# Audio tower with experts: opening loads and fold re-ordered, shared expert's down products moved by one chunk

## The chip, the cores and the metric

One core of one Trainium2 chip runs the whole program. The metric is the device time of one execution in microseconds (us). TensorE (PE in the rows) multiplies, VectorE (DVE), ScalarE (ACT) and GpSimd (POOL) do the rest, SyncE (SP) only issues transfers. ACT and POOL can issue transfers too.

## The reference, cut to what matters

32 audio clips give 250 frames each, so 8000 tokens of 192 numbers.

```python
h = tok(x)                       # |rfft(frame)|^2 @ mel -> log -> @ dct @ w_proj + b_proj
h = h + attn(layernorm(h))       # 8 heads, softmax(q k^T + relative-position bias) v, then a gelu MLP
xn = layernorm(h)
scores = sigmoid(xn @ gate.T)    # 8000 x 16
topk_score, topk_ids = top_k(scores.T, 1000)     # each of 16 experts picks its 1000 best tokens
xg = xn[topk_ids]
out = (silu(xg @ Wg.T) * (xg @ Wu.T)) @ Wd.T * topk_score     # hidden width 768
y = zeros.at[topk_ids].add(out)
shared = (silu(xn @ Ws_g.T) * (xn @ Ws_u.T)) @ Ws_d.T         # hidden width 384
return h + y + shared
```

## The kernel before, in words

Every engine has a program of its own, written out by hand in order. A semaphore is a counter: `then_inc` raises it, `wait_ge` holds the engine, and all that is queued behind on that engine, until a value is reached.

**The tower** (`tower`) runs 32 batches of 250 tokens as a pipeline of five stages; `body(bt, bq, bb_, bc, bd)` is one round with up to five batches in flight, each in eight slots `s`. Stage `bt` is the front end: spectrum (`dft`, slot 1), mel filter (`mel`, slot 2), log, projection (`wmel`, slot 4), layer norm and rms norm (slots 5 and 6), a transpose and a split into a high and a low part, `hsp` (slot 7). Stage `bq` forms q, k, v (`qk`, first matmuls of the next round) and the position terms `rsb`, which SP stores into `bias_d`. That tensor is filled with zeros beforehand, and the first store waits for it (`zero_st`).

Before the first round stands an opening. SP loads `frames` of batch 0, waits for three memsets of POOL, and issues 40 loads on one semaphore, `w_ld`. All other engines wait for all of them (`W_LOADS`). Then come:

- the high half of the weight split on ACT (`wsp` from `wraw`, two operations of 1600 columns) and the low half on DVE;
- the fold on PE: `wqT` by `wpz` (32 half-array matmuls recorded at L742), `dct` by `wproj` into `wmel`, and `wpz` by `vcol` into `cq`;
- four small high copies on ACT and four low ones on DVE of the folded columns.

After `ini` has reached 9, PE starts the spectrum of batch 0.

**The feed-forward part** (`feed_forward`) has 16 chunks of 500 tokens for the shared expert. In a chunk PE does three units (`m`): a gate and an up product, five matmuls each, into the PSUM tiles `gps` and `ups`, two buffers each. ACT takes the silu, DVE multiplies (`gated`) into `s_hT`. Then PE does 24 down matmuls (two groups of 12) from `s_hT` into `dps`, and DVE adds the residual (`added`). ACT then issues the store of the result. The split of the next chunk's input is `high` on ACT and `low` on DVE.

In chunks 0 to 9 the same engines search the 16 thresholds of the top 1000 bit by bit, three steps a chunk. `count` is a DVE pass over 128x1000 scores, `tally` a small matmul that sums it over partitions, `update` three short DVE operations that need the tally. In chunks 10 to 15 (`SEARCH` is 10) `route` turns the thresholds into index lists: prefix sums by a scan on DVE with a matmul behind it on PE (`route(c, 4)`), then `one_hots` on DVE, `list_mm` on PE, `list_out` on DVE. SP stores the list (`store_list`) and loads it back, POOL gathers 1000 rows by eight indirect transfers (`gather`), and PE transposes them (`rows_T`), with `rows_high` on ACT and `rows_in` on DVE, for the first of 16 experts. In SP's own order the store of list 0 stands behind all transfers of the chunks, and the last of those waits for `added(13)`.

After that come 16 turns of an expert each.

## Time and profile before

| what | value |
|---|---|
| three runs | 2084.29, 2087.18, 2087.20 us; median 2087.18 |
| the profiled execution, its own time | 2081.72 us |
| its span, first to last instruction | 2080.1 us |
| busy: PE, DVE, ACT, POOL | 92%, 66%, 51%, 34% of the span |
| opening, until the first q/k matmul | 0 to 46.5 us |
| tower | to about 1088 us |
| shared expert and routing, chunks 0 to 15 | 1094.3 to 1299.7 us |
| first expert's rows | 1299.7 to 1314.1 us |
| 16 expert turns | 1314.1 to 2080 us |

All stages follow one another on PE, so the span is their sum. A busy share over the whole span says little about one stage: what an edit is worth is read inside its stage, from who waits for whom.

### The profile page before, as it was taken

The page shows a single profiled execution, that of the slowest core. Times are in us where ns is not written, and L with a number is a line of the kernel's source. Part 1 is how long each engine was busy: PE and PEld are TensorE (multiplying, and loading weights), DVE is VectorE, ACT ScalarE, POOL GpSimd, SP SyncE. Part 2 cuts the span into 40 slices and gives each one's busy share as a digit, 9 for nine tenths or more (in the row PEclk, how much of TensorE's full clock was granted, in tenths as well). Part 3 has the DMA queues.
Part 4 walks back from the last instruction along what each step waited for, and adds up shares of the span by engine and source line. Part 5 has one row for each costly group of instructions (what it writes and reads, how often), then busy time and mean ns, then how long its engine had stood idle before and what let it go on. Part 6 is the DMA issues. An engine that isn't in the chain of part 4 may idle for free. (4 is left out here: it accounts for less than half of the span.)

```text
span 2080.1 us, 46488 instructions
## 1 busy us (share of the span) xinstructions
PE 1912.6 (92%) x13428; PEld 1634.6 (79%) x13428; DVE 1364.8 (66%) x3748; ACT 1070.9 (51%) x2588; POOL 704.5 (34%) x587
## 2 busy tenths in 40 slices
PE   2899999999999999999958899799999999999997
PEld 2688888888888888888847787688888888888886
DVE  2577878878878878878746777455555555555531
ACT  2687787887887887887732221222222222222221
POOL 0122222222222222212210002266666665566663
PEclk9999999999999999999979999899999999999999
DMA  5666666666766666666636333244454554444451
GB/s 154 167 164 174 186 172 173 188 170 172 191 168 172 193 166 175 188 167 178 189 89 164 98 99 90 64 81 82 82 93 83 99 99 83 79 78 81 81 95 19
DMA packets 318048, 272.95 MB, mean 131 GB/s; under 512 B 80732, under 2 KB 305326, under 8 KB 317998
## 3 DMA queue, kind: packets, MB, share of 16 engines
q1 hardware_dynamic: 238878, 235.53, 42.1%
q0 software_dynamic: 70656, 30.65, 10.2%
q10 hardware_dynamic: 8464, 6.15, 0.9%
q8 instruction: 26, 0.43, 0.1%
q14 instruction: 24, 0.20, 0.0%
HBM read 151.25 MB, written 120.54 MB: 131 GB/s over the span
## 5 line engine op out<-in xcount | busy, mean ns | idle before, releaser
L1211 POOL DMA_INDIRECT out<-ff_y,ff_idxs x128 | 261.8, 2045 | 232.7 <-DVE ff_y L1490 175.0
L1266 ACT ACTIVATE ff_sg<-ffp_g 128x500 f32<-128x500 f32 x192 | 113.0, 589 | 384.5 <-PE ffp_g L1602 384.5
L1198 POOL DMA_INDIRECT ff_xg<-xs_d,ff_idxg x128 | 206.3, 1612 | 284.4 <-issue 269.4
L524 ACT ACTIVATE sb_prob<-sb_ssb,sb_mx 125x250 f32<-125x250 f32 x512 | 253.3, 499 | 61.0 <-DVE sb_rinv L614 33.1
L1614 PE MATMUL ffp_d<-ff_wd,ff_wide 128*125 128x192 f32 x1536 | 261.2, 327 | 7.7 <-DVE ff_wide L1477 6.7
L1477 DVE TENSOR_TENSOR ff_wide<-ff_sg,ffp_u 128x500 f32<-128x500 f32 x192 | 129.4, 674 | 207.9 <-PE ffp_u L1602 207.9
L1602 PE MATMUL ffp_g<-ff_xsp,ff_wsp 128*128 128x500 f32 x960 | 250.8, 391 | 7.6 <-issue 6.0
L1614 PEld LDWEIGHTS ffp_d<-ff_wd,ff_wide 128*125 128x125 f32 x1536 | 247.8, 188 | 11.2 <-issue 9.1
L1602 PE MATMUL ffp_u<-ff_xsp,ff_wsp 128*128 128x500 f32 x960 | 250.1, 390 | 0.0
L1602 PEld LDWEIGHTS ffp_g<-ff_xsp,ff_wsp 128*128 128x128 f32 x960 | 180.1, 189 | 45.3 <-issue 9.5
L822 PE MATMUL ps_qps<-sb_hsp,sb_wsp 128*128 128x250 f32 x1280 | 184.5, 291 | 32.0 <-DVE sb_hsp L728 22.8
L1602 PEld LDWEIGHTS ffp_u<-ff_xsp,ff_wsp 128*128 128x128 f32 x960 | 181.4, 189 | 37.2
L822 PEld LDWEIGHTS ps_qps<-sb_hsp,sb_wsp 128*128 128x128 f32 x1280 | 159.5, 191 | 56.8 <-ACT sb_rsb L510 28.2
L608 DVE CUSTOM_DVE_ANT_0 sb_ssb<-ps_sps,sb_bsk 125x250 f32<-125x250 f32 x512 | 192.0, 412 | 10.1 <-PE ps_sps L773 3.2
L510 ACT ACTIVATE sb_rsb<-ps_qps 125x502 f32<-125x502 f32 x256 | 137.0, 590 | 80.4 <-PE ps_qps L844 66.2
L587 DVE COPY sb_ptsb<-ps_ptps 125x500 f32<-125x500 f32 x256 | 170.8, 667 | 5.0 <-PE ps_ptps L784 3.0
L784 PE MATMUL ps_ptps<-sb_ident,sb_prob 125*125 125x125 f32 x1024 | 154.8, 273 | 2.3 <-ACT sb_prob L524 1.4
L773 PE MATMUL ps_sps<-sb_kk,sb_qu 64*125 64x250 f32 x1024 | 143.3, 398 | 0.2
L455 POOL TENSOR_TENSOR sb_t_y<-sb_t_v,sb_power 125x4 f32<-125x4 f32 x32 | 33.0, 1032 | 323.8 <-DVE sb_t_v L711 323.8
L784 PEld LDWEIGHTS ps_ptps<-sb_ident,sb_prob 125*125 125x125 f32 x1024 | 136.9, 188 | 5.1 <-ACT sb_prob L524 2.6
L1241 ACT ACTIVATE ff_xsp<-ffp_tp 128x500 fp32r<-128x500 f32 x64 | 37.6, 587 | 175.7 <-PE ffp_tp L1525 175.7
L1490 DVE TENSOR_SCALAR ff_y<-ffp_d,ff_gsc 125x192 f32<-125x192 f32 x128 | 47.5, 413 | 119.3 <-PE ffp_d L1614 119.3
(190 smaller groups left out, 3528.0 us busy)
## 6 DMA issues: line engine op xcount, KB each, us to landing
bias_d<-sb_rsb SPq DMA_DIRECT2D x256, 219.6 KB
sb_bsk<-bias_d SPq DMA_DIRECT2D x256, 218.8 KB
hx_d<-sb_hx SPq DMA_DIRECT2D x32, 336.0 KB
sb_hxl<-hx_d SPq DMA_DIRECT2D x32, 336.0 KB
ff_wd<-WdT SPq DMA_DIRECT2D x16, 576.0 KB, 5.0
xs_d<-sb_xs SPq DMA_DIRECT2D x32, 238.0 KB
bias_d<-sb_rsb SPq DMA_DIRECT2D x256, 25.5 KB
sb_bsk<-bias_d SPq DMA_DIRECT2D x256, 25.4 KB
```

The lines of the kernel that those rows point to most:

```text
L510: a.activation(rsb[:, h % 2], bank2(qps[R_USE[h] % 2], NDE, TP)[:, :, 0:ND], ACT.Copy).then_inc(q_ev[R_USE[h] % 2], 2)
L524: a.activation(prob[:, s % 2, t], ssb[:, s % 2, t], ACT.Exp, bias=mx[:, s % 2, t:t + 1], scale=-1.0, accum_out=rs[:, t, s:s + 1]).then_inc ...
L587: v.tensor_copy(ptsb[:, h % QUAD], ptps[:]).then_inc(pt_ev, 1)
L608: v.tensor_tensor_reduce(out=ssb[:, s % 2, t], in0=sps[s % 2][:, t], in1=bsk[:, s % 4, t], scale=-SCALE, scalar=3.0e38, op0=ALU.add, op1=A ...
L773: ins = m(sps[i][:, t], qu[rows, p, t * TP:(t + 1) * TP], kk[rows, p], start=True, stop=True)
L784: ins = nc.tensor.transpose(ptps[:, j, t * TP:(t + 1) * TP], prob[:, h % 2, t, j * TP:(j + 1) * TP], ident[0:TP, 0:TP])
L822: ins = m(ps[:, i], wsp[:, wk, col:col + 128], hsp[:, xp, xk], start=k == 0, stop=k == len(PARTS) - 1)
L1198: g.indirect_dma_start(xg[:, t], None, xs_d[:, :], bass.IndirectOffsetOnAxis(idxg[:, t:t + 1], 0), bounds_check=last).then_inc(gat, 16)
L1211: g.indirect_dma_start(out_d[:, :], bass.IndirectOffsetOnAxis(idxs[:, t:t + 1], 0), y[:, t], None, bounds_check=last, compute_op=ALU.add). ...
L1477: v.tensor_tensor(hT[:, m, half * HALF:(half + 1) * HALF], sg[:, n % 2], ups[n % 2][:], ALU.mult).then_inc(h_ev, 1)
L1602: ins = m_(ps[n % 2][:], wsp[:, i, wk, m * 128:(m + 1) * 128], xsp[:, xp, xk, half * HALF:(half + 1) * HALF], start=k == 0, stop=k == 4)
L1614: ins = m_(dps[j % 2][:, i], hT[:, m, t * TP:(t + 1) * TP], wd[:, m], start=m == 0, stop=m == ME - 1)
```

## The change

In the opening the loads fall into four semaphores: `f_ld` (`dft`), `t_ld` (what the first front end reads), `w_ld` (weights to be split and folded) and `l_ld` (what only later stages read). Twelve loads of `wq`, `wk`, `wv`, `w1` become three of one array, `wall`, joined on the host. ACT issues 12 loads itself. The front end of batch 0 starts when its own few loads are there; the weight split and the fold stand behind its steps on each engine. The fold's PSUM tiles are `cps` and `otps` in place of `tps` and `cps`. The zero stores stand behind all loads, the POOL memset of `zeros` behind the others.

In the feed-forward part `down(c-1)` stands behind the first unit of chunk c, `added(c-1)` and the store with it, and DVE's order within a chunk is another. `list_mm` and some `one_hots` move. The first expert's four transposed groups get four PSUM tiles (`rows_ps`).

The diff, cut to its core:

```diff
@@ tower, SP @@
+            loads = [(wraw[:, 0], w["wall"][0:128])] + [(wraw[64 * i:64 * i + 64, 1], w["wall"][128:D]) for i in range(2)]
+            ...  braw x4, ucol;   late = wo, w2, gate, n2w, b1, bb x4
             load_frames(0)
-            sp.wait_ge(z_set, 3)
+            sp.dma_start(mel[0:BINS], w["melT"]).then_inc(t_ld, 16)
+            sp.dma_start(mel[BINS:2 * BINS], w["melT"]).then_inc(t_ld, 16)
+            sp.wait_ge(z_set, 2)
             for dst, src in loads:
                 sp.dma_start(dst, src).then_inc(w_ld, 16)
+            sp.wait_ge(t_mm, 1)
+            load_frames(1)
+            for dst, src in late:
+                sp.dma_start(dst, src).then_inc(l_ld, 16)
+            sp.wait_ge(z_set, 7)
@@ tower, ACT @@
+            act.dma_start(dft[:], w["dft"]).then_inc(f_ld, 16)
+            ...  dct, wproj, wmel on t_ld;  wqT, vcol, wpz x4 on w_ld;  ident, n1w on t_ld
             a.preload_act_table_set(EXP_SET)
-            act.wait_ge(w_ld, W_LOADS)
             act.wait_ge(z_set, 7)
...
                         a.activation(hx[:, :, 0:D], bank2(tps, D, TP), ACT.Copy).then_inc(t_ev, 1)
+                        if opening(bt):
+                            weights_high()
@@ tower, DVE: weights_low() behind h1n @@
+                        if opening(bt):
+                            weights_low()
@@ tower, PE @@
                         m(tps[0:2 * BINS, 0:FRAMES], dft[:], frames[:], start=True, stop=True).then_inc(t_mm, 1)
+                        if opening(bt):
+                            mel_fold()
...
                         ins.then_inc(t_mm, 1)
+                        if opening(bt):
+                            fold()
@@ tower, PE, qk of batch 0 @@
+                    if opening(b):
+                        pe.wait_ge(ini, 8)
@@ feed_forward, first expert's rows @@
+            if isinstance(e, int) and e == 0:
+                return (tp, gps[0], gps[1], ups[0])[j][:, 0:HALF].rearrange("p (t n) -> p t n", n=TP)
@@ feed_forward, ACT, chunk @@
-                if not last:
-                    high(c + 1, 1 - par)
+                    if m == 0 and (not isinstance(c, int) or c < CHUNKS - 1):
+                        high(c + 1, 1 - par)
+                    if m == 0 and (not isinstance(c, int) or c > 0):
+                        stored(c - 1, 1 - par)
@@ feed_forward, DVE, chunk @@
+                    if c == SEARCH:
+                        update(STEPS * c - 1)
+                    route(c, 0)
+                    if c < CHUNKS - 1:
+                        low(c + 1, 1 - par)
+                    if c == SEARCH + 4:
+                        list_out(0)
+                    added(c - 1, 1 - par)
+                    gated(c, par, 0)
+                    for m in range(1, MS):
                         route(c, m)
                         gated(c, par, m)
                     route(c, 3)
-                    if c < CHUNKS - 1:
-                        low(c + 1, 1 - par)
-                    added(c, par)
                 else:
+                    if not first:
+                        update(STEPS * c - 1)
                     count(STEPS * c)
-                    gated(c, par, 0)
                     update(STEPS * c)
                     count(STEPS * c + 1)
+                    low(c + 1, 1 - par)
+                    if not first:
+                        added(c - 1, 1 - par)
+                    if first:
+                        gated(c, par, 0)
+                    update(STEPS * c + 1)
+                    if not first:
+                        gated(c, par, 0)
+                    count(STEPS * c + 2)
                     gated(c, par, 1)
-                    update(STEPS * c + 1)
                     gated(c, par, 2)
-                    count(STEPS * c + 2)
-                    low(c + 1, 1 - par)
-                    update(STEPS * c + 2)
-                    added(c, par)
@@ feed_forward, PE, chunk, behind unit m @@
                     if search and m == 0:
                         tally(STEPS * c)
+                    if not search and c == SEARCH + 4 and m == 0:
+                        list_mm(0)
+                    if m == 0 and not first:
+                        down(c - 1)
+                    if search and m == first:
+                        tally(STEPS * c + 1)
                     if search and m == 2:
-                        tally(STEPS * c + 1)
+                        tally(STEPS * c + 2)
                     if not search:
                         route(c, m)
-                pe.wait_ge(s_h_ev, MS * (c + 1))
-                ...  24 down matmuls
                 if not search:
                     route(c, 4)
```

DVE in the opening, before: the split and the fold's copies (`sb_wsp`, `sb_bz`, `sb_cq`) lead, the norm of batch 0 (`sb_t_stats` and on) follows.

```order
L569 CAST sb_bz<-sb_braw 128x504
L572 TENSOR_TENSOR sb_wsp<-sb_wraw,sb_wsp 128x1600
L572 TENSOR_TENSOR sb_wsp<-sb_wraw,sb_wsp 64x1600
L574 COPY sb_cq<-ps_qps 128x4
L575 COPY sb_wmel<-ps_qps 40x192
L579 TENSOR_TENSOR sb_wsp<-ps_tps,sb_wsp 128x4x32
```

And of the change, from the last part of that norm to the split of batch 0's `hsp`:

```order
L759 TENSOR_SCALAR sb_h1n<-sb_hx,sb_t_y 125x64
L604 CAST sb_bz<-sb_braw 128x504
L607 TENSOR_TENSOR sb_wsp<-sb_wraw,sb_wsp 128x1600
L607 TENSOR_TENSOR sb_wsp<-sb_wraw,sb_wsp 64x1600
L609 COPY sb_cq<-ps_qps 128x4
L613 TENSOR_TENSOR sb_wsp<-ps_cps,sb_wsp 128x4x32
L613 TENSOR_TENSOR sb_wsp<-ps_otps,sb_wsp 128x4x32
L613 TENSOR_TENSOR sb_wsp<-ps_cps,sb_wsp 64x4x32
L613 TENSOR_TENSOR sb_wsp<-ps_otps,sb_wsp 64x4x32
L766 SCALAR_TENSOR_TENSOR sb_hsp<-ps_tps,sb_n1w,sb_hsp 128x250 x2
```

The whole split now stands between `h1n` and `hsp` of batch 0.

PE at the end of chunk 10, the first behind the search, before: units 1 and 2 (`ffp_g`, `ffp_u`), the down products (`ffp_d`), then the prefix matmul (`ff_before`), then chunk 11.

```order
L1567 MATMUL ffp_g0<-sh_s_xsp,sh_s_wsp 128x500 x5
L1567 MATMUL ffp_u0<-sh_s_xsp,sh_s_wsp 128x500 x5
L1580 MATMUL ffp_d0<-sh_s_wd,ff_s_hT 125x192 x6
L1580 MATMUL ffp_d1<-sh_s_wd,ff_s_hT 125x192 x6
L1542 MATMUL ffp_kl<-ff_wide,ff_before 128x1
L1567 MATMUL ffp_g1<-sh_s_xsp,sh_s_wsp 128x500 x5
```

And of the change:

```order
L1648 MATMUL ffp_g0<-sh_s_xsp,sh_s_wsp 128x500 x5
L1648 MATMUL ffp_u0<-sh_s_xsp,sh_s_wsp 128x500 x5
L1618 MATMUL ffp_kl<-ff_wide,ff_before 128x1
L1648 MATMUL ffp_g1<-sh_s_xsp,sh_s_wsp 128x500 x5
L1648 MATMUL ffp_u1<-sh_s_xsp,sh_s_wsp 128x500 x5
L1635 MATMUL ffp_d0<-sh_s_wd,ff_s_hT 125x192 x6
```

The prefix matmul now follows unit 2 at once; the down products of chunk 10 stand behind it and behind the first unit of chunk 11.

DVE from the end of chunk 13 into chunk 14, before (`ff_lst` and `ff_lsti` are `list_out(0)`, `ff_y` is `added(13)`, `sh_s_xsp` is `low(14)`):

```order
L1334 TENSOR_TENSOR ff_val<-ff_one_lo,ff_tile 125x64x32
L1310 TENSOR_TENSOR sh_s_xsp<-sh_s_xraw,sh_s_xsp 128x500 x2
L1317 TENSOR_TENSOR ff_y<-ffp_d0,ff_res 125x384
L1317 TENSOR_TENSOR ff_y<-ffp_d1,ff_res 125x384
L1341 COPY ff_lst<-ffp_kl 32x64
L1344 TENSOR_TENSOR ff_lst<-ffp_kl,ff_lst 32x64 x3
```

And of the change (`sh_s_xsp` is now `low(15)`):

```order
L1399 TENSOR_TENSOR ff_val<-ff_one_lo,ff_tile 125x64x32
L1375 TENSOR_TENSOR sh_s_xsp<-sh_s_xraw,sh_s_xsp 128x500 x2
L1406 COPY ff_lst<-ffp_kl 32x64
L1409 TENSOR_TENSOR ff_lst<-ffp_kl,ff_lst 32x64 x3
L1412 SCALAR_TENSOR_TENSOR ff_lsti<-ff_lst 32x32
L1382 TENSOR_TENSOR ff_y<-ffp_d0,ff_res 125x384
L1382 TENSOR_TENSOR ff_y<-ffp_d1,ff_res 125x384
```

`added(13)` now stands behind `list_out(0)` and waits for the down products behind it on PE. SP's order at this place is the same in both kernels.

## Rows read from the trace of the kernel before

**Rows 1.** Windows: busy us per engine, granted clock, DMA share, GB/s.
```profile
0.00:25.00 25.00, 0.00 (x0) 0.00 (x0) 0.00 (x0) 1.28 (x1) 2.43 (x11) 1.00 0.56 148
```

**Rows 2.** Timeline of the opening: start, us, engine, line, operation.
```profile
21.41 1.73 SPq L349 DMA_DIRECT2D sb_wraw<-w  x3
23.19 7.04 SPq L353 DMA_DIRECT2D bias_d<-sb_zeros  x5
25.24 2.96 ACT L470 ACTIVATE sb_wsp<-sb_wraw 128x1600 fp32r<-128x1600 f32 x2 [23.08 <-DMA sb_wraw<-w]
26.81 3.68 DVE L572 TENSOR_TENSOR sb_wsp<-sb_wraw,sb_wsp 128x1600 fp32r<-128x1600 f32 x2 [1.15 <-ACT sb_wsp L470]
29.60 1.87 PE L745 MATMUL ps_qps<-sb_vcol,sb_wpz 128*128 128x1 f32 x8
```

**Rows 3.** Timeline: the first front end and the first q/k product.
```profile
33.40 1.16 PE L866 MATMUL ps_tps<-sb_frames,sb_dft 100*102 100x250 f32 x2 [1.93 <-DVE sb_wsp L579]
...
35.02 1.06 PE L872 MATMUL ps_tps<-sb_sq,sb_mel 102*40 102x250 f32 x2 [0.47 <-ACT sb_sq L528]
...
38.48 0.49 ACT L546 ACTIVATE sb_hx<-ps_tps 125x384 f32<-125x384 f32 x1 [0.43 <-PE ps_tps L897]
...
43.25 0.26 DVE L723 TENSOR_SCALAR sb_h1n<-sb_hx,sb_t_y 125x64 f32<-125x64 f32 x1
...
45.56 0.86 DVE L728 SCALAR_TENSOR_TENSOR sb_hsp<-ps_tps,sb_n1w,sb_hsp 128x250 fp32r<-128x250 f32 x2 [2.05 <-ACT sb_hsp L560]
46.47 2.21 PEld L822 LDWEIGHTS ps_qps<-sb_hsp,sb_wsp 128*128 128x128 f32 x10 [2.21 <-DVE sb_hsp L728]
...
53.26 13.16 SPq L98 DMA_DIRECT2D bias_d<-sb_rsb  x12
```

**Rows 4.** Windows: the first 2.5 us behind the loads, zero stores running.
```profile
25.00:27.50 2.50, 2.24 (x22) 2.24 (x22) 1.11 (x2) 2.26 (x2) 0.00 (x0) 1.00 0.99 271
```

**Rows 5.** Transfers by line: KB each, median us to landing.
```profile
bias_d<-sb_zeros SPq DMA_DIRECT2D x5, 779.7 KB, 10.8
sh_s_xraw<-xnT_d SPq DMA_DIRECT2D x16, 250.0 KB, 4.4
```

**Rows 6.** Waits, chunks 1 to 9: us in total, times, longest.
```profile
PE ffp_d L1580 <- DVE ff_s_hT L1304: 11.6, 9, 1.3
```

**Rows 7.** Timeline of PE: one search chunk and the next one's start.
```profile
1199.67 1.44 PE L1567 MATMUL ffp_g<-sh_s_xsp,sh_s_wsp 128*128 128x500 f32 x5
...
1208.48 2.21 PE L1580 MATMUL ffp_d<-sh_s_wd,ff_s_hT 128*125 128x192 f32 x12 [1.32 <-DVE ff_s_hT L1304]
...
1212.56 1.43 PE L1567 MATMUL ffp_g<-sh_s_xsp,sh_s_wsp 128*128 128x500 f32 x5
```

**Rows 8.** Timeline of DVE: a count and a prefix scan.
```profile
1105.75 1.25 DVE L1289 TENSOR_SCALAR_CACHE_REDUCE ff_wide<-ff_wide,ff_cand 128x1000 f32<-128x1000 f32 x1
...
1233.41 2.23 DVE L1383 TENSOR_TENSOR_SCAN ff_wide<-ff_wide 128x1000 f32<-128x1000 f32 x1
```

**Rows 9.** Timeline of PE: first matmuls of chunks 1, 10 and 14.
```profile
1109.79 1.43 PE L1567 MATMUL ffp_g<-sh_s_xsp,sh_s_wsp 128*128 128x500 f32 x5
...
1225.41 1.43 PE L1567 MATMUL ffp_g<-sh_s_xsp,sh_s_wsp 128*128 128x500 f32 x5
...
1275.32 1.41 PE L1567 MATMUL ffp_g<-sh_s_xsp,sh_s_wsp 128*128 128x500 f32 x5
```

**Rows 10.** Timeline, SP, POOL, PE: list 0, its gather, the first expert's rows.
```profile
1276.68 0.34 SPq L1145 DMA_DIRECT2D idx_d<-ff_lsti  x1
...
1283.27 3.36 POOL L1198 DMA_INDIRECT ff_xg<-xs_d,ff_idxg  x1 [194.80 <-issue]
...
1286.93 1.32 POOL L1198 DMA_INDIRECT ff_xg<-xs_d,ff_idxg  x1 [0.30 <-issue]
...
1303.79 1.07 PE L1525 MATMUL ffp_tp<-ff_ident,ff_xg 125*128 125x125 f32 x4 [4.04 <-DMA ff_xg<-xs_d,ff_idxg]
...
1314.08 2.42 PE L1602 MATMUL ffp_g<-ff_xsp,ff_wsp 128*128 128x500 f32 x5 [1.55 <-DVE ff_xsp L1354]
```

More of the change, by code:

```diff
@@ L205, in tower @@
         zero_st = sem("zero_st")
+        t_ld = sem("t_ld")
+        f_ld = sem("f_ld")
+        l_ld = sem("l_ld")
+        mel_mm = sem("mel_mm")
+        mel_in = sem("mel_in")
         fold_mm = sem("fold_mm")
@@ L736, in _, with mel_fold, fold @@
             m = nc.tensor.matmul
-            pe.wait_ge(w_ld, W_LOADS)
-            for p in range(PAIRS):
-                for k in range(2):
-                    for i in range(2):
-                        rows = slice(64 * i, 64 * i + 64)
-                        m(folded(i, k)[:, p], wqT[rows, p, k * 128:(k + 1) * 128], wpz[rows, p, 0, i], start=True, stop=True)
-            m(qps[1][0:MELS, 0:D], dct[:], wproj[:], start=True, stop=True)
-            for p in range(PAIRS):
-                ins = m(qps[0][:, p:p + 1], wpz[:, p].rearrange("d r i n -> d (r i n)"), vcol[:, p:p + 1], start=True, stop=True)
-            ins.then_inc(fold_mm, 1)
-            pe.wait_ge(ini, 9)
-            pe.wait_ge(z_set, 7)
+            pe.wait_ge(f_ld, 16)
+            pe.wait_ge(z_set, 7)
+            def mel_fold():
+                pe.wait_ge(t_ld, T_LOADS)
+                m(qps[1][0:MELS, 0:D], dct[:], wproj[:], start=True, stop=True).then_inc(mel_mm, 1)
+            def fold():
+                pe.wait_ge(w_ld, W_LOADS)
+                for p in range(PAIRS):
+                    for k in range(2):
+                        for i in range(2):
+                            rows = slice(64 * i, 64 * i + 64)
+                            m(folded(i, k)[:, p], wqT[rows, p, k * 128:(k + 1) * 128], wpz[rows, p, 0, i], start=True, stop=True)
+                for p in range(PAIRS):
+                    ins = m(qps[0][:, p:p + 1], wpz[:, p].rearrange("d r i n -> d (r i n)"), vcol[:, p:p + 1], start=True, stop=True)
+                ins.then_inc(fold_mm, 1)
             def transposes(ps, src, s):
@@ L1240, in rows_high, with stored @@
                 k, half = j % 2, j // 2
-                a.activation(xsp[:, 0, k, half * HALF:(half + 1) * HALF], tps.rearrange("p t n -> p (t n)"), ACT.Copy).then_inc(t_hi, 1)
+                a.activation(xsp[:, 0, k, half * HALF:(half + 1) * HALF], rows_ps(e, j).rearrange("p t n -> p (t n)"), ACT.Copy).then_inc(t_hi, 1)
+            def stored(c, par):
+                act.wait_ge(s_y_ev, 2 * c + 2)
+                sprayed(act, out_d[bass.ds(c * CHUNK, CHUNK), :].rearrange("(t p) n -> p t n", p=TP), y[:, CT * par:CT * par + CT], y_st[par])
             def chunk(c, par):
-                last = isinstance(c, int) and c == CHUNKS - 1
                 for m in range(MS):
@@ L1551, in route, with down @@
                     places(1)
-                if c == SEARCH + 3 and place == 4:
-                    list_mm(0)
-                if c == SEARCH + 5 and place == 4:
-                    list_mm(1)
+            def down(c):
+                pe.wait_ge(s_h_ev, MS * (c + 1))
+                for i in range(2):
+                    wait(pe, s_y_ev, 2 * (c - 1) + i + 1)
+                    for t in range(2):
+                        for m in range(MS):
+                            ins = m_(dps[i][:, t], s_hT[:, m, (2 * i + t) * TP:(2 * i + t + 1) * TP], s_wd[:, m], start=m == 0, stop=m == MS - 1)
+                    ins.then_inc(s_d_mm, 1)
             def chunk(c, par):
@@ L1587, in _ @@
             chunks(pe, chunk)
+            down(CHUNKS - 1)
+            list_mm(1)
             pe.wait_ge(r_ch, 13)
```

147 lines of the change are left out of this document (82 added, 65 removed).

## The prediction

> **What bounds the kernel now.** I read the windows first, then the timeline of the opening, then the waits, the timelines and the chain of waits from chunk 0 to the first expert. PE is the engine to follow: in the tower's rounds and in the expert turns it is nearly always busy and the diff leaves both as they are, so what stands ahead of them shifts them one for one. Three places are left.
>
> The opening. For 25 us no compute engine does anything but memsets while the transfers move 148 GB/s [rows 1], though they move 271 GB/s as soon as large ones queue [rows 4]. So the opening waits for SP's issues: the last weight load is issued at 21.41 and three issues take 1.73, 0.58 us each; everything starts at 25.24 [rows 2]. The weight work then takes until 33.40, the front end until 46.47 [rows 3].
>
> The chunks. In chunks 1 to 9 PE waits once a chunk, ahead of the down products, for the last product of that chunk: 11.6 us in nine times [rows 6]. The row at 1208.48 shows 1.32 of it, in a chunk of 12.89 us (1199.67 to 1212.56) [rows 7].
>
> The first expert's rows. List 0 is stored at 1276.68, the gather starts at 1283.27, its rows reach PE at 1303.79, and the first expert product starts at 1314.08 [rows 10]. PE's chunk work has ended at about 1299.7. The last wait there is the transfer of the gathered rows, so from here back the chain runs over POOL and SP, not over PE.
>
> **Term 1, the opening.** The first front end now needs only its own loads (`t_ld`). ACT issues 12 loads, the last of them on `t_ld`; at 0.5 us each (0.58 in rows 2 is for large ones) from 0.9 they are out at 7. A transfer of 250 KB lands 4.4 us after its issue [rows 5]; these are small but share the engines with `wall`, so 3.5: landed at 10.5. Bounds: 9, if nothing is in the way; 13, if they land behind all 2.6 MB of `t_ld` and `w_ld` together, which at 271 GB/s [rows 4] take 9.6 us from about 2.5, plus a landing of about 1. A page warns of the upper one: the Trainium skill, "DMA: Bandwidth & Descriptors", section "Issuing engines are not separate DMA queues", says that two issuing engines share the same 16 transfer engines and save only issue time. By that sentence alone the sum would be 2.5 us later.
>
> From `t_ld` on: `mel_fold` and its copy 1.2 (estimate, one small matmul of 1.06 as at 35.02 less overlap, and a DVE copy); mel matmul to `hx` 3.46 (35.02 to 38.48); `hx` to the end of `h1n` 5.03 (38.48 to 43.51) [rows 3]. Then DVE does what it did ahead: cast 0.4, low split 3.68 [rows 2], the folded columns. For these I have the bound of 1.9 (from the fold's end at 31.5 [rows 2] to 33.40 [rows 3], ACT's part included) and take 1.2, since ACT's part is done by then. Last `hsp` to the first q/k product, 0.91 [rows 3]. Sum 15.9: the product starts at 26.4 instead of 46.47, **20.1 us less**. ACT's high split (2.96) and PE's fold (25.26 to 31.5) [rows 2] start when `hx` is formed and end 6 to 7 us later, under DVE's 10 us: free. `w_ld` may land as late as 15.7 at no cost.
>
> The zero stores are issued after that, by 18 us, and need 14.4 us for 3.9 MB at 271 GB/s [rows 4]; one lands 10.8 us after issue [rows 5]. They end near 30. The first `rsb` store needs them 6.8 us behind the first q/k product (46.47 to 53.26) [rows 3], at 33.2. Covered, by 3 us only.
>
> **Term 2, search chunks.** Without its wait a chunk is 12.89 - 1.32 = 11.57 us of PE [rows 7]. What is late next: the first tally stands ahead of the down products, and its count comes on DVE behind the last `gated` (0.6), the last `update` (about 0.6) and the pass of 1.25 [rows 8]. Counted from the chunk's first matmul it is there at 2.70; PE has done unit 0 at 2.41 and waits 0.3. The chain after it (update, count, `low`, `added`, update, `gated`, count, `gated`) ends at 10.8 by the same durations, ahead of unit 2's end. Chunk: 11.7 to 11.85, so 1.1 less. Chunk 0 loses its down products to chunk 1 (4.1 and the wait) but pays 1.4, because `gated(0)` stands behind `low(1)` and its transfer: chunk 1 starts at 1105.8 instead of 1109.79 [rows 9]. Over chunks 1 to 9, 10.0 to 10.5. Chunk 10 starts at 1211.4 instead of 1225.41 [rows 9]; 4 of the 14 are only postponed.
>
> **Term 3, routing chunks.** Chunks 10 to 13 took 49.9 us [rows 9]. Now the prefix matmul of chunks 10 and 11 follows unit 2 directly, and it needs `gated(c, 2)` (0.6) and the scan (2.2 [rows 8]) first; the down products, which hid the scan, come after. PE waits 3.0 us twice, where it waited 0.77. A chunk without tallies is 11.15: 14.25 + 14.15 + 11.9 (transposes) + 11.1 = 51.4. **The gain shrinks here**: chunk 14 starts at 1262.8 instead of 1275.32.
>
> **Term 4, the first expert.** In chunk 14 unit 0 ends at 2.4, `list_mm(0)` waits for the last one-hot until 3.0 and ends at 3.7, `down(13)` ends at 7.65 and `added(13)` at 8.3. SP has the store of list 0 queued behind the residual load of chunk 15, which waits for `added(13)`; so the list, formed by 5.4, is stored at 9.4 and not at 1.4 as before. That is 1272.2 against 1276.68, 4.5 us less. Store to rows is 27.1 us (1276.68 to 1303.79) [rows 10] and nothing in it changes: rows at 1299.3. PE is through with chunk 15 at about 1293 and waits 6 us; whatever PE gained beyond 4.5 us, and the delay of `gated(15, 2)` by a one-hot of 2.2, is lost or hidden there. The four groups then run in four PSUM tiles: instead of 10.29 us (1303.79 to 1314.08) PE, ACT and DVE overlap, 1.1 + 0.6 + 4 x 0.7 + 0.3 = 4.9. First expert product at 1304.2: **9.9 us less** for terms 2 to 4 together.
>
> **Sum.** 20.1 + 9.9 = 30.0. The profiled execution took 2081.72, its span 2080.1, so it would be 2051.7. It was 5.5 us below the median of the three runs (2087.18), which gives 2057; I say **2056**.
>
> **Rivals.**
> - Search chunks stay near 12.9 us because the ring count, tally, update closes on DVE and PE in turn. For it: DVE's work in a chunk is nearly 10 us and four of its steps wait for PE. Against: 1 us of slack as counted. Then store and rows come 10 us later, 20 us less in all: 2067. Chance 0.11.
> - The opening gives only about 11: loads land at 13 and later, or the zero stores end past 33 and hold the first bias. 2066. The transfer rows [rows 4, 5] leave 3 us to that. Chance 0.12.
> - The gather is shorter. The record at 1283.27 took 3.36, the next 1.32 [rows 10]; the long one began while a one-hot of 2.3 us ran on DVE, and there are two such. If the one-hots of chunk 15 fall beside it: 3.9 less, 2052. I count both again inside the gather, so chance 0.12. The Trainium skill, "SBUF — State Buffer", section "Who interferes with whom", infers that a `tensor_tensor` of DVE does not hold descriptor writing on GpSimd; the rows look otherwise, and the rows decide.
> - Nothing gained: the opening ends later for a load I count as free and the chunks give back the rest, within 4 us of now. I find no row for it: 0.03.
> - Slower: the input load of chunk c+2 is issued only behind `added(c-1)`, and the ring is load, `high`, `low`, `added`, again load. I count 9.5 us with a landing of 4.4 [rows 5]. It binds from a landing of 6.6; each us more costs one per chunk. To eat 30 us over ten chunks it must be 9.6: the same transfer would have to land twice as late. 2095. Chance 0.02.
>
> The forecast itself, 26 to 33 us less, has 0.60. So faster by over 0.2% (4 us, about what a measurement of this kernel can tell) 0.94, within it 0.03, slower 0.03. Range 2048 to 2066: the lower end takes the short gather and the early loads with 4 us of spread between runs, the upper the two costlier rivals.
>
> **What would show it.** First q/k matmul near 26.4 (9 to 13 for the loads makes 24.9 to 28.9), with its last wait on DVE's `hsp`. Zero stores landed ahead of the first `rsb` store. Chunk to chunk 11.7 in the search; the wait of `ffp_d` for `ff_s_hT` gone, one of `ffp_kl` for DVE's count of 0.3 in its place. PE waits of 3 us ahead of the prefix matmuls of chunks 10 and 11. Store of list 0 about 9.4 us into chunk 14, PE idle 6 us ahead of the first expert's rows, and 5 us from the rows to its first product. Wrong if the first tally or the zero stores wait for microseconds, or if rows come by another chain than store, load back, gather.

## The result, and the profile after

Four runs of each kernel: the change 2068.03 us median (2067.60 to 2070.41), before 2085.73 (2082.90 to 2087.20), ratio 0.9919, 95% interval 0.9902 to 0.9936. That is 17.7 us less where 30 were forecast, and above the range. The profiled execution of the change took 2068.2 us, its span 2066.5; against the 2051.7 that the sum gave for a profiled execution it is 16.5 us too long. The profiled execution of before lies 5.5 us below the median of its first three runs, that of the change at its own median. So the two traces differ by 13.6 us where the medians differ by 17.7: the times say what the change is worth, the traces say where.

The opening, timeline of the change (start, us, engine, line, operation, and in brackets idle time and what ended it). It answers to [rows 2, 3]:

```profile
3.81 5.05 ACTq L485 DMA_DIRECT2D sb_wpz<-w_pos  x4
8.90 1.75 ACTq L486 DMA_DIRECT2D sb_ident<-ident  x1
10.68 0.65 ACTq L487 DMA_DIRECT2D sb_n1w<-n1w  x1
...
19.33 0.85 PE L780 MATMUL ps_qps<-sb_wproj,sb_dct 13*40 13x192 f32 x2 [14.66 <-DMA sb_n1w<-n1w]
...
34.59 2.46 PE L867 MATMUL ps_qps<-sb_hsp,sb_wsp 128*128 128x250 f32 x10 [5.05 <-DVE sb_hsp L766]
...
41.49 0.79 SPq L98 DMA_DIRECT2D bias_d<-sb_rsb  x2
```

And its windows (busy us of PE, PEld, DVE, ACT, POOL, granted clock, DMA share, GB/s), against [rows 1]:

```profile
5.00:7.50 2.50, 0.00 (x0) 0.00 (x0) 0.00 (x0) 0.00 (x0) 0.00 (x0) 1.00 1.06 294
7.50:10.00 2.50, 0.00 (x0) 0.00 (x0) 0.00 (x0) 0.00 (x0) 0.00 (x0) 1.00 1.05 190
10.00:12.50 2.50, 0.00 (x0) 0.00 (x0) 0.00 (x0) 1.13 (x1) 0.00 (x0) 1.00 1.03 185
```

ACT's last two loads, `ident` (64 KB) and `n1w` (1 KB), are among those that the first front end needs, and they are issued at 8.9 and 10.7 us, behind four issues of 1.26 each. `t_ld` is complete 8 us behind the last of them, while the 16 transfer engines are full (share above 1; that this is the cause is shown by `e10_free` below). The trace names `n1w`, the last one issued, as what ended the wait; `ident` stands just ahead on the same semaphore and may have landed last. From `t_ld` on the sum holds: 15.3 us to the first q/k product (15.9 forecast), 6.9 from there to the first `rsb` store.

From chunk 0 to the first expert, the longest waits of PE (us in total, times, longest):

```profile
PE ffp_tp L1601 <- DMA ff_xg<-xs_d,ff_idxg: 4.4, 1, 4.4
PE ffp_kl L1618 <- DVE ff_wide L1448: 3.0, 1, 3.0
PE ffp_kl L1621 <- DVE ff_wide L1460: 2.9, 1, 2.9
PE ffp_kl L1583 <- DVE ff_wide L1354: 2.9, 9, 0.5
PE ffp_d L1635 <- DVE ff_s_hT L1369: 2.7, 1, 2.7
PE ffp_u L1648 <- DVE ff_s_hT L1369: 2.4, 1, 2.4
```

The nine waits of up to 1.3 of [rows 6] are gone, nine of 0.3 on average stand in their place, as forecast. New and not forecast is the 2.4 in chunk 1. Its timeline shows a transfer behind it:

```profile
1093.14 0.59 SPq L1202 DMA_DIRECT2D ff_wd<-WdT  x1
1094.16 0.34 SPq L1217 DMA_DIRECT2D sh_s_xraw<-xnT_d  x1
1095.04 1.17 SPq L1219 DMA_DIRECT2D sh_s_xraw<-xnT_d  x2
...
1105.21 1.13 ACT L1288 ACTIVATE sh_s_xsp<-sh_s_xraw 128x500 fp32r<-128x500 f32 x2 [7.24 <-DMA sh_s_xraw<-xnT_d]
...
1109.07 1.75 PE L1648 MATMUL ffp_u<-sh_s_xsp,sh_s_wsp 128*128 128x500 f32 x5 [2.37 <-DVE ff_s_hT L1369]
```

The input of chunk 2 is issued behind five constants and 2.1 MB of expert weights that SP loads in chunk 1, and lands 9 us after its last issue. In the order of before nothing on PE hung on it so early; now `low(2)` stands ahead of `added(0)` and `gated(1, 0)` on DVE.

The routing chunks, and the end of the feed-forward part, against [rows 9, 10]:

```profile
1221.34 0.35 PE L1618 MATMUL ffp_kl<-ff_wide,ff_before 128*128 128x1 f32 x2 [3.01 <-DVE ff_wide L1448]
1221.55 1.59 PE L1648 MATMUL ffp_g<-sh_s_xsp,sh_s_wsp 128*128 128x500 f32 x5
1222.94 2.29 PE L1648 MATMUL ffp_u<-sh_s_xsp,sh_s_wsp 128*128 128x500 f32 x5
...
1237.46 2.43 PE L1648 MATMUL ffp_g<-sh_s_xsp,sh_s_wsp 128*128 128x500 f32 x5
...
1262.44 1.30 PE L1648 MATMUL ffp_g<-sh_s_xsp,sh_s_wsp 128*128 128x500 f32 x5
...
1270.98 0.83 SPq L98 DMA_DIRECT2D ff_res<-h_d  x2
1271.86 0.35 SPq L1206 DMA_DIRECT2D idx_d<-ff_lsti  x1
1278.29 3.01 POOL L1259 DMA_INDIRECT ff_xg<-xs_d,ff_idxg  x1 [200.05 <-issue]
1281.61 1.31 POOL L1259 DMA_INDIRECT ff_xg<-xs_d,ff_idxg  x1 [0.30 <-issue]
...
1297.70 1.07 PE L1601 MATMUL ffp_tp<-ff_ident,ff_xg 125*128 125x125 f32 x4 [4.42 <-DMA ff_xg<-xs_d,ff_idxg]
1302.79 1.38 PE L1683 MATMUL ffp_g<-ff_xsp,ff_wsp 128*128 128x500 f32 x5 [1.55 <-DVE ff_xsp L1419]
```

A group of five products takes 1.3 us at full clock and 2.3 to 2.4 behind the 3-us waits. There the windows show half of the clock granted, 1.2 instead of 2.4 GHz:

```profile
1237.50:1241.70 4.20, 4.20 (x11) 3.43 (x12) 2.74 (x5) 1.60 (x3) 0.00 (x0) 0.50 0.00 0
```

Chunk 14 starts 178.5 us behind the start of chunk 0, where before took 181.0 and 168.5 were forecast. The list is stored 9.4 us into chunk 14, as forecast to a tenth; rows to first product 5.1 (4.9 forecast, 10.3 before).

### The profile page after: what moved, and what is told of

It reads as the page before. It is cut to its first block and busy times, and to the rows that moved or that the text cites. A ratio compares the mean times of both kernels' runs of the same rounds, so it can differ in the third digit from the quotient of the medians.

```text
span 2066.5 us, 46500 instructions
## 1 busy us (share of the span) xinstructions
PE 1919.8 (93%) x13428; PEld 1642.8 (79%) x13428; DVE 1364.0 (66%) x3748; ACT 1071.7 (52%) x2588; POOL 700.3 (34%) x587
## 3 DMA queue, kind: packets, MB, share of 16 engines
q0 software_dynamic: 70656, 30.65, 10.3%
## 5 line engine op out<-in xcount | busy, mean ns | idle before, releaser
L1695 PEld LDWEIGHTS ffp_d<-ff_wd,ff_wide 128*125 128x125 f32 x1536 | 247.8, 188 | 14.2 <-issue 13.0
```

The costliest lines, as they stand in the source:

```text
L1695: ins = m_(dps[j % 2][:, i], hT[:, m, t * TP:(t + 1) * TP], wd[:, m], start=m == 0, stop=m == ME - 1)
```

## The experiments

Before, the change and 15 further kernels in one table. The times (us) are of each profiled execution: `t_ld` complete, first q/k product, first `rsb` store, start of chunk 0, then counted from chunk 0: list 0 stored, first rows on PE, first expert product. The ratio to before goes by several executions of each kernel, run side by side; in parentheses stands its 95% interval.

| kernel | t_ld | q/k | rsb | chunk 0 | list | rows | expert | ratio |
|---|---|---|---|---|---|---|---|---|
| before | - | 46.5 | 53.3 | 1094.3 | 182.3 | 209.4 | 219.7 | 1 |
| the change | 19.3 | 34.6 | 41.5 | 1083.9 | 187.9 | 213.8 | 218.9 | 0.9919 |
| e1e_open | 19.6 | 34.9 | 42.1 | 1087.8 | 182.5 | 207.2 | 217.1 | 0.9955 (0.9941 to 0.9970) |
| e2e_shared | - | 46.6 | 53.3 | 1094.1 | 185.8 | 211.6 | 216.7 | 0.9987 (0.9976 to 0.9998) |
| e15_down | - | 46.7 | 53.6 | 1096.6 | 188.5 | 214.3 | 224.5 | 1.0023 (1.0011 to 1.0034) |
| e9_tiles | 18.9 | 34.2 | 41.1 | 1082.7 | 188.5 | 213.4 | 222.5 | 0.9953 (0.9940 to 0.9966) |
| e3e_first | 15.6 | 30.9 | 38.1 | 1084.2 | 189.0 | 214.8 | 219.8 | 0.9912 (0.9894 to 0.9931) |
| e4e_hold | 18.8 | 34.1 | 43.2 | 1087.7 | 188.8 | 213.7 | 217.6 | 0.9923 (0.9908 to 0.9937) |
| e11_rows | 15.0 | 30.3 | 37.7 | 1080.0 | 188.7 | 214.4 | 219.4 | 0.9904 (0.9886 to 0.9922) |
| e10_free | 4.9 | 26.0 | 37.9 | 1079.5 | 185.9 | 211.7 | 216.7 | 0.9890 (0.9876 to 0.9905) |
| e13_zero | 4.9 | 25.9 | 32.9 | 1078.0 | 185.6 | 211.3 | 216.3 | 0.9888 (0.9870 to 0.9906) |
| e5_input | 20.4 | 35.6 | 42.6 | 1085.0 | 184.4 | 209.3 | 213.2 | 0.9916 (0.9902 to 0.9929) |
| e6_prefix | 20.3 | 35.6 | 42.7 | 1088.9 | 179.7 | 205.7 | 210.8 | 0.9886 (0.9869 to 0.9903) |
| e7_list | 19.8 | 35.0 | 41.9 | 1087.0 | 185.0 | 213.1 | 217.3 | 0.9918 (0.9904 to 0.9931) |
| e8_all | 15.7 | 30.9 | 37.8 | 1083.2 | 171.5 | 196.6 | 200.8 | 0.9834 (0.9818 to 0.9850) |
| e12_best | 14.2 | 29.5 | 37.4 | 1082.7 | 171.0 | 195.8 | 199.7 | 0.9809 (0.9796 to 0.9822) |
| e14_best | 4.9 | 25.6 | 32.3 | 1073.5 | 171.1 | 195.8 | 199.7 | 0.9805 (0.9787 to 0.9822) |

### Which part gave what

`e1e_open` and `e2e_shared` each take one of the two functions from the change:

```diff
@@ e1e_open: tower and host arrays of the change, feed_forward of before @@
@@ e2e_shared: tower and host arrays of before, feed_forward of the change @@
```

> Before's feed-forward part behind the change's tower: the opening alone. Theory (the parts add): the first q/k product starts near 34.6 us and chunk 0 near 1084 instead of 1094.3, and nothing behind it moves, so 10.4 us less than before, ratio 0.995. Rival (the opening's gain is partly lost again later, since zero stores and late loads disturb the tower): less than 8 us. Rival (the other part owns most of the gain): within 3 us of before.

> Before's tower in front of the change's feed-forward part: the shared expert, the lists and the four PSUM tiles alone. Theory: first expert product 0.9 us less after the start of chunk 0 and expert turns 2.3 us shorter through the warmer clock, so 3 us less than before, ratio 0.9985, with the input wait of chunk 1 (it takes 14.9 instead of 12) and the half clock in the routing chunks as in the change. Rival (the change's feed-forward part is worth the 9.9 us of the forecast, and the earlier opening cost it the rest): 8 to 10 us less, ratio near 0.996.

`e9_tiles` is the change without the four PSUM tiles, `e15_down` the same feed-forward part behind the tower of before:

```diff
-            if isinstance(e, int) and e == 0:
-                return (tp, gps[0], gps[1], ups[0])[j][:, 0:HALF].rearrange("p (t n) -> p t n", n=TP)
             return tps
@@ PE, ahead of each group @@
-                if not isinstance(e, int) or e > 0:
-                    pe.wait_ge(t_ev, TR * e + j)
+                wait(pe, t_ev, TR * e + j)
```

> The change with the first expert's four transposed groups back in one PSUM tile, in turn. Theory (within the feed-forward part the four tiles carry the gain, and the moved down products by themselves bring the rows no earlier): rows to first expert product 10.3 instead of 5.1 us, and its first products at half clock again, 5 to 7.5 us more than the change: ratio to before 0.9950. Rival (the tiles give little, because ACT and DVE set the pace of the split): at most 2 us more, ratio below 0.993.

> Before's tower, and the change's feed-forward part with the first expert's rows back in one PSUM tile: the moved down products, list and one-hots alone. Theory (what they gain in the search chunks they give back in chunks 1 and 10 to 12 and in the late store of the list): rows as in e2b_shared, 2 us later than before relative to chunk 0, 2 to 4 us slower than before, ratio 1.0015. Rival (they are worth what the ratios of the change, of the opening alone and of the change without the tiles leave, nothing): ratio 0.9995 to 1.0005. Rival (as forecast, 5 us faster without the tiles): 0.9975.

The opening alone gives 0.9955 (0.995 expected), the feed-forward part 0.9987 (0.9985 expected): both first theories hold. The interval of `e1e_open` reaches to 0.9970, so its rival of less than 8 us (0.9962) is unlikely and not excluded. The tiles are worth what 0.9953 and 0.9919 differ by, 7 us, and again 7.5 between 1.0023 and 0.9987. The end of `e15_down`:

```profile
1310.95 0.99 PE L1543 MATMUL ffp_tp<-ff_ident,ff_xg 125*128 125x125 f32 x4 [4.36 <-DMA ff_xg<-xs_d,ff_idxg]
1313.40 1.09 PE L1543 MATMUL ffp_tp<-ff_ident,ff_xg 125*128 125x125 f32 x4 [1.46 <-DVE ff_xsp L1362]
...
1321.16 2.42 PE L1625 MATMUL ffp_g<-ff_xsp,ff_wsp 128*128 128x500 f32 x5 [1.55 <-DVE ff_xsp L1362]
```

10.2 us from rows to first product, and that product at half clock, as in [rows 10]. So the moved down products, with the lists and one-hots moved along, make the kernel **slower**, by 0.23%: PE's search chunks are shorter, but the list is stored 6 us later relative to chunk 0, and the rows hang on the list.

### Why t_ld was late

`e3e_first` issues `ident` and `n1w` ahead of the weights; `e4e_hold` leaves ACT's order as in the change and holds SP's late loads until `t_ld` is complete.

```diff
@@ e3e_first, ACT @@
+            act.dma_start(ident[:], w["ident"]).then_inc(t_ld, 16)
+            act.dma_start(n1w[:], w["n1w"]).then_inc(t_ld, 16)
             act.wait_ge(z_set, 1)
             act.dma_start(wqT[:], w["wqT"].rearrange("(p r) n -> r p n", r=128)).then_inc(w_ld, 16)
@@ e4e_hold, SP (alone) @@
             load_frames(1)
+            sp.wait_ge(t_ld, T_LOADS)
             for dst, src in late:
```

> The change, with ident and n1w issued by ACT ahead of wqT, vcol and the four wpz loads. Theory A (the small loads of the first front end came late because they stood at the end of ACT's own order): they are out by 3.8 us, t_ld is complete near 13, the weights (w_ld) near 20 are next, and the first q/k product starts at 28 to 30 instead of 34.6: 5 us less than the change, ratio to before 0.9895. Theory B (all 16 transfer engines were full and the order of issue does not matter): t_ld complete at 17 or later, at most 2 us less than the change.

> The change, with SP holding its nine late loads back until t_ld is complete; ACT's order is left. Theory C (the late loads of SP, issued from 7.6 us on, took the transfer engines from n1w): t_ld complete near 15 instead of 19.3, first q/k product near 30.5, 4 us less than the change, ratio to before 0.990. Theory A (ACT's order alone): t_ld still near 19, and the zero stores, now issued behind it, end some 5 us later, near 41, where the first rsb store is due at 41.5: same as the change, or up to 2 us slower.

`e10_free` adds to `e3e_first` a wait for `t_ld` ahead of all weight loads; `e11_rows` adds to `e3e_first` one transfer for `wpz` instead of four; `e13_zero` is `e10_free` with the zero stores first.

```diff
@@ e10_free, ACT and SP @@
             act.wait_ge(z_set, 1)
+            act.wait_ge(t_ld, T_LOADS)
...
             sp.wait_ge(z_set, 2)
+            sp.wait_ge(t_ld, T_LOADS)
             for dst, src in loads:
@@ e11_rows, ACT @@
-            for i in range(2):
-                for r in range(2):
-                    act.dma_start(wpz[64 * i:64 * i + 64, :, r, i], ...).then_inc(w_ld, 16)
+            act.dma_start(wpz[:], w["w_pos"].rearrange("q (p r i n) -> q p r i n", p=PAIRS, r=2, i=2)).then_inc(w_ld, 16)
@@ e13_zero, SP: the loop over late stands behind the zero stores @@
```

> The change with ident and n1w first, and all transfers of w_ld (SP's and ACT's) held back until t_ld is complete. Theory (what the first front end reads lands late because the 16 transfer engines are full of weights): t_ld complete at 6 to 8 us instead of 15.6 with the order alone, then w_ld near 20 to 22 is the last wait, the first q/k product at 29 to 31: same time as with the order alone. Rival (these small loads are slow by themselves, each with its own fixed cost): t_ld complete at 12 or later.

> The change with ident and n1w first, and wpz loaded in one transfer with its zeros, 128 rows of 2 KB from an array that the host pads, instead of four transfers of 256 pieces of 128 bytes. Theory (the small pieces hold the transfer engines at 190 GB/s where they could move 290): t_ld complete near 12 instead of 15.6, w_ld near 16 instead of 19.9, first q/k product 27.5 instead of 30.9, 3 us less than with the order alone. Rival (wall and wqT fill the engines, the small pieces are 0.13 MB of 2.6): less than 1 us.

> As e10_free (ident and n1w first, weights held back until t_ld is complete), with SP issuing the zero stores ahead of the nine late loads. Theory (with the first q/k product at 26 the zero stores are the next wait: the first rsb store went 11.9 us behind it instead of 6.9): they are issued near 11 instead of 17.8, the first rsb store goes near 33 to 34 instead of 37.9, and the time is 3 to 4 us less than e10_free, ratio to before 0.987. Rival (the zero stores share the engines with the weights, w_ld lands later and the q/k product with it): first q/k product near 29, first rsb store 36, at most 1.5 us less than e10_free.

Order alone brought `t_ld` from 19.3 to 15.6, in `e3e_first`:

```profile
15.58 0.85 PE L780 MATMUL ps_qps<-sb_wproj,sb_dct 13*40 13x192 f32 x2 [10.84 <-DMA sb_n1w<-n1w]
```

That lies between its two theories (13, and 17 or later). The first q/k product came 3.7 us earlier, but the time moved from 0.9919 to 0.9912 only, less than the intervals can tell and far from the 0.9895 expected. Holding SP's late loads left `t_ld` at 18.8, at the edge of what six traces with the same order of ACT's loads show without that hold (18.9 to 20.4), and its first `rsb` store went 1.7 us later than that of the change. One transfer for the small pieces of `wpz` gave 0.6 us (15.0), and 1.4 in `e12_best` (14.2) against `e8_all` (15.7): the first theories of both fell. The last small load of `e3e_first` was issued at 3.0, and `t_ld` still took 12 us more. With the engines free (`e10_free`) it is complete at once:

```profile
4.87 0.86 PE L782 MATMUL ps_qps<-sb_wproj,sb_dct 13*40 13x192 f32 x2
...
11.06 1.05 PE L923 MATMUL ps_tps<-sb_sq,sb_mel 102*40 102x250 f32 x2 [5.34 <-ACT sb_sq L556]
...
17.59 2.96 ACT L496 ACTIVATE sb_wsp<-sb_wraw 128x1600 fp32r<-128x1600 f32 x2 [2.58 <-DMA sb_ucol<-u]
...
17.78 8.35 SPq L363 DMA_DIRECT2D bias_d<-sb_zeros  x5
...
25.95 2.46 PE L869 MATMUL ps_qps<-sb_hsp,sb_wsp 128*128 128x250 f32 x10 [1.98 <-DVE sb_hsp L768]
...
37.86 1.69 SPq L98 DMA_DIRECT2D bias_d<-sb_rsb  x4
```

So the small loads were late because of the megabytes on their way beside them: that is what the theory of full engines said (6 to 8 us expected, 4.9 measured). The weights lose nothing by starting 3 us later (`w_ld` complete at 17.6, 19.9 in `e3e_first`). There the theory was too careful: it had `w_ld` at 20 to 22 and the product no earlier than with the order alone, and the first q/k product starts at 25.95, 4.9 us ahead of `e3e_first` and 20.5 ahead of before. Of the 14.5 us by which `t_ld` is ahead of the change, 8.6 reach that product. The row at 11.06 shows where most of the rest goes: ACT now issues its weight loads, until 9.3 us, ahead of its first step of the front end, and PE waits 5.3 us for that step. Then the zero stores are late: the first `rsb` store goes 11.9 us behind the product instead of 6.9. `e13_zero` mends that:

```profile
10.56 6.05 SPq L361 DMA_DIRECT2D bias_d<-sb_zeros  x5
...
25.94 2.47 PE L869 MATMUL ps_qps<-sb_hsp,sb_wsp 128*128 128x250 f32 x10 [1.98 <-DVE sb_hsp L768]
...
32.85 6.96 SPq L98 DMA_DIRECT2D bias_d<-sb_rsb  x8
```

The store goes 5 us earlier, as its theory said, but chunk 0 starts only 1.5 us earlier, and the time does not tell the two apart (0.987 expected). The first rounds of the tower, which take the rest back, are below, under the hardware.

### The chunks

```diff
@@ e5_input, SP, chunk: input of chunk c+1 right behind the residual load of chunk c @@
                 sprayed(sp, res[:, par], h1_d[own, :].rearrange("(t p) n -> p t n", p=TP), r_ld[par])
+                if not isinstance(c, int) or c < CHUNKS - 1:
+                    load_x(c + 1, 1 - par)
                 if isinstance(c, int) and c == 1:
@@ e6_prefix, PE, chunk, behind unit m @@
+                    if m == 0 and not search and c - 1 in (SEARCH, SEARCH + 1):
+                        route(c - 1, 4)
                     if m == 0 and not first:
                         down(c - 1)
...
-                if not search:
-                    route(c, 4)
@@ e7_list, SP, chunk @@
+                if isinstance(c, int) and c == CHUNKS - 1:
+                    store_list(0)
+                    load_idx(idxg, ig_ld, 0)
                 wait(sp, s_y_ev, 2 * (c - 1))
```

> The change, with SP issuing the input of chunk c+1 right behind the residual load of chunk c, so that the input of chunk 2 no longer stands behind the constants and expert weights that SP loads in chunk 1; all else as in the change. Theory (chunk 1 waits 2.4 us and then runs at half clock because that input is issued late): chunk 1 takes 12 instead of 14.9 us, chunks 2 to 9 stay at 11.95, 3 us less than the change, ratio to before 0.9905. Rival (the expert weights take the transfer engines wherever they stand, or the wait moves to DVE's chain): chunk 1 above 14, no change in time.

> The change, with the two prefix matmuls of chunks 10 and 11 behind the first unit of the next chunk and ahead of its down products. Theory (PE waits for DVE's scan only for what no work covers, and each 3-us wait is followed by half-clock products): the two waits fall from 3.0 to 0.5 us, no product of chunks 10 to 13 is at half clock, chunks 10 to 13 take 46 instead of 55.3 us, the list is stored 9 us earlier, the first expert starts 9 us earlier: ratio to before 0.9875. Rival (DVE is the bound of the routing chunks): chunks 10 to 13 take 51 or more, at most 4 us less. Rival (the waits were 3 us but the half clock does not follow from them): 50.

> The change, with SP storing list 0 and loading it back ahead of the residual load of chunk 15, which waits for added(13). Theory (the store is held by SP's order, the list is formed 4 us before): store 5.4 us into chunk 14 instead of 9.4, rows 4 us earlier, PE idle ahead of them 0.4 instead of 4.4 us, 4 us less than the change, ratio to before 0.990. Rival (the list itself is late, DVE forms it behind the wait for the last one-hot): store not before 8 us, at most 1.5 us less.

`e5_input`: chunk 1 takes 11.92 us, the wait is gone, and from chunk 0 to the first expert it is 5.7 us less than the change, of which 3.0 are this wait. By the times it is 0.9916 against 0.9919 (0.9905 expected), so the 3 us are shown in the trace and not in the time.

`e6_prefix`, timeline of PE:

```profile
1227.05 0.35 PE L1618 MATMUL ffp_kl<-ff_wide,ff_before 128*128 128x1 f32 x2 [0.74 <-DVE ff_wide L1448]
...
1238.85 0.38 PE L1621 MATMUL ffp_kl<-ff_wide,ff_before 128*128 128x1 f32 x2 [0.64 <-DVE ff_wide L1460]
```

Waits of 0.7 instead of 3.0, no product at half clock, chunks 10 to 13 in 46.4 us instead of 55.3 (46 expected). DVE is not the bound there. The time shows it: 2062.76, ratio 0.9886 against 0.9919, 7 us less (9 expected), with intervals that overlap by 0.0001 only.

`e7_list`:

```profile
1271.94 0.35 SPq L1206 DMA_DIRECT2D idx_d<-ff_lsti  x1
...
1276.01 1.63 POOL L1260 DMA_INDIRECT ff_xg<-xs_d,ff_idxg  x1 [194.68 <-issue]
1279.81 3.18 POOL L1260 DMA_INDIRECT ff_xg<-xs_d,ff_idxg  x1 [0.30 <-issue]
...
1292.34 7.12 PE L1636 MATMUL ffp_d<-sh_s_wd,ff_s_hT 128*125 128x192 f32 x24 [2.73 <-DVE ff_s_hT L1370]
1300.02 0.65 PE L1602 MATMUL ffp_tp<-ff_ident,ff_xg 125*128 125x125 f32 x4
```

The list is stored 5.5 us into chunk 14 (1266.42), and the gather starts 4.1 behind it instead of 6.4. PE no longer waits for the rows, but its last 24 down products took 7.1 us, most of it at half clock, instead of 4.2. They stand behind the wait of 2.7, which the change has too, and PE itself became the end of the chain. The first expert product comes 1.6 us earlier relative to chunk 0 where 4 were expected, and the time is that of the change: the store came as the theory said, its gain did not.

### Together

`e8_all` holds the edits of `e3e_first`, `e5_input`, `e6_prefix` and `e7_list`. `e12_best` adds that of `e11_rows` and moves a one-hot; `e14_best` adds those of `e10_free` and `e13_zero`.

```diff
@@ e12_best, DVE, route, chunk 15 @@
                     if place == 1 or place == 2:
                         weights_low(0, place + 1)
-                        one_hots(1, place + 1)
+                    if place == 1:
+                        one_hots(1, 2)
+                    if place == 3:
+                        one_hots(1, 3)
```

> The four edits together: ident and n1w first, input of chunk c+1 behind the residual of chunk c, prefix matmuls behind the next first unit, list 0 ahead of the last residual load. Theory (they lie on one path and add): 3.7 + 3 + 9 + 4 = 20 us less than the change, near 2048, ratio to before 0.983. Rival (with the list early and PE's chunks shorter, PE or the gather takes over, one of the last two is lost): near 2052, ratio 0.985.

> The four edits of e8_all, the wpz load in one transfer, and the last one-hot of chunk 15 behind gated(15, 2) instead of ahead of it. Theory: PE's wait ahead of the last down products falls from 2.7 to 0.5 us, the first expert starts 1 us earlier (the rows are next), the opening 3 us earlier: near 2045, ratio to before 0.9815. Rival (only the opening, or nothing, comes through): 2047 to 2050.

> e12_best with the opening of e13_zero. Theory: the openings add to the rest, first q/k product at 26 instead of 29.5 and first rsb store 4 us earlier, near 2042, ratio to before 0.979. Rival (the opening's further gain goes to the clock episode between 50 and 65 us or to the zero stores): 2045 to 2047.

The four edits together give what their theory said: 2049.23 us, 0.9834 (0.983 expected), 18 us less than the change. One by one the times had shown only 1.5, 0.6, 7 and 0.2 us, 9 in all; each of these is a difference of two ratios that are known to about 3 us each, so the times one by one can neither show nor deny that the edits add. In the traces, from chunk 0 to the first expert product, `e5_input`, `e6_prefix` and `e7_list` gain 5.7, 8.1 and 1.6 us one by one, and the four together 18.1. The missing 2.7 fits an early list that PE could not use in `e7_list` alone, and is not tested by itself. `e12_best` has 2046.16 and 0.9809 (0.9815 expected); PE's wait ahead of the last down products fell from 2.7 to 0.8. `e14_best` has 2043.06 us against 2084.18 of before in the same comparison, the fastest of all. Its first q/k product at 25.6 us is 4 us ahead of `e12_best`, while the ratios differ by 0.0004: its expectation (0.979) lies in the interval, and so does its rival.

## Why the prediction was wrong

Against its own sum for a profiled execution, 2051.7, the change is 16.5 us late: 8.2 in term 1, 1.5 in the tower, 9.0 in terms 2 to 4, and 2.3 given back in the expert turns.

**Term 1 failed at one step: "so 3.5: landed at 10.5".** It took a landing time from a transfer on nearly idle engines and scaled it by size. The upper bound was the right mechanism (they land behind what is queued), but at 271 GB/s where the windows from 7.5 to 12.5 us show 185 to 190, and it took ACT's issues at 0.5 us each where four of them took 1.26. Measured: 19.3, 6 us beyond the bound. The Trainium skill, "DMA: Bandwidth & Descriptors", section "Issuing engines are not separate DMA queues", says that loads of all issuing engines run on the same 16 transfer engines. The traces agree: 8 to 12 us from the issue of the last small load to `t_ld`, at a DMA share of about 1.05, and under 2 us with those engines free. All else of term 1 held: 15.3 us from `t_ld` to the product, DVE as its last wait, the fold and the high split hidden, and the zero stores covered here, by little: with the product at 26 (`e10_free`) they end near 37.8 and not near 30 as counted, so the prediction's own 26.4 would have hit them. Its own terms, issued by 18 us and 14.4 us of transfer, already add up to 32.4 and not 30.

**Term 2.** The new wait of 0.3 and its place were right. Of the 6.1 us missing at the start of chunk 10, 3.2 are chunk 1, where the prediction counted the ring load, `high`, `low` with a landing of 4.4 us and did not look at what SP has ahead of that load in chunk 1 (shown by `e5_input`). The last of its rivals had nearly this price, "It binds from a landing of 6.6; each us more costs one per chunk": the landing was 9.0 and the wait 2.4, in one chunk instead of ten. Of the rest, 0.8 us is the half clock behind that wait, in chunk 2, 0.6 is chunk 0, and 0.2 is lost in each further chunk, 11.95 instead of 11.73, a term mis-sized.

**Term 3** had both 3-us waits, to 0.1 us, and left out the clock: chunks 10 to 13 took 55.3 us instead of 51.4, 3.9 more. "PE waits 3.0 us twice" was priced as the waits alone; the products behind them ran at 1.2 GHz in part, in chunks 11 (15.9 us, 14.15 counted) and 12 (14.3, 11.9 counted). `e6_prefix` shows that without the waits none does. The 12.5 us that chunk 14 was to start earlier relative to chunk 0 became 2.5.

**Term 4** held: store at +9.4, 5.1 from rows to product, the one-hot that delays `gated(15, 2)`, PE idle 4.4 (6 forecast). The rival of a shorter gather came in part: 25.8 us from store to rows instead of 27.1, with 3.01, 1.74 and 1.99 where 1.29 is the rule. In all traces the records of 2.7 us and more begin beside a one-hot of 2.3 on DVE and end 1.2 us behind its end, as if they had stood still until then (1278.29 + 3.01 = 1281.30, the one-hot ends at 1280.06). The Trainium skill, "SBUF — State Buffer", section "Who interferes with whom", infers that a `tensor_tensor` does not hold descriptor writing, and for these indirect transfers the rows do not agree with it. The same section says that a DVE instruction with two SBUF inputs contends with a GpSimd instruction that reads SBUF. The one-hots have two such inputs and the gather takes its indices from SBUF (`ff_idxg`), which would fit; no run here tells the two apart. What was not seen at all: first products at full clock after four overlapped groups (1.38 and 1.30 instead of 2.42 and 2.29), 2.0 of the 2.3 us of the expert turns. The tiles alone do not settle it: `e6_prefix` has the same four and 2.42 us again, and turns 1.5 us longer than the change.

The rival "the opening gives only about 11", at 0.12, came true (11.9). By itself it would have given 2066, the upper end of the range; the 9 us of terms 2 to 4 came on top. The rival on the search chunks has about that size, but its mechanism did not come: those chunks took 11.95 us and not 12.9. What took its place, chunk 1 and the clock behind the waits, stood in no rival as it came, and the prediction let its rivals come one at a time only.

**What stays open.** The parts don't close: opening alone 0.9955, moved products 1.0023 and tiles 0.9966 give 0.9944, the change has 0.9919, 5 us less. The intervals reach that far, and the clock episodes below differ between executions by nearly as much; no run here settles it. Nor is the 1.5 us in the tower explained.

## What to carry to other kernels

Here the landing time of a small load was set by the bytes on their way on both queues: give the first consumer's loads free engines and hold the rest back, then look for the next user of the same engines (here the zero stores). When a step is moved, follow every issue queue that it now waits on, at the first iterations too, where one-time loads stand between. Price a wait on PE of 3 us together with the slower products that may follow it, and ask of each earlier step whether the chain that ends last (here the list) became earlier: the moved products alone made this kernel slower.
